# Convolutions in rounds of sixteen tiles, weights fused inside the recurrence, and TensorE's waits at the first weight load

## The reference

```python
x = x + L0(_gn(x))        # a bidirectional LSTM along one image axis, then a linear layer
x = x + L1(_gn(x))        # three convolutions joined: plain, and two with learned offsets
```

```python
out_standard = conv2d(x, conv_w, conv_b, padding=1)                     # 3x3, 32 -> 32 channels
h = relu(batchnorm(conv2d(x, dw_w, dw_b, padding=1, groups=32)))        # once for x, once for y
offset = conv2d(h, pw_w, pw_b)                                          # 32 -> 9 offsets a pixel
out_x, out_y = (einsum('bchwk,ock->bohw', bilinear_samples(x, offset), weight) for x and y)
out = relu(batchnorm(conv2d(concatenate([out_standard, out_x, out_y]), fus_w)))   # 96 -> 32, 1x1
```

## Time and profile before

| what | us |
|---|---|
| time before, median of three runs | 897.43 (894.85 to 897.92) |
| the profiled execution's own time | 896.58 |
| its span, first to last instruction | 894.1 |
| TensorE matmuls busy | 772.6 (86%) |
| VectorE busy | 615.6 (69%) |
| ScalarE busy | 478.8 (54%) |
| GpSimd busy | 249.4 (28%) |
| TensorE on the chain that ended last | 67% |

### The profile page before, as it was taken

How to read it: one execution, slowest core, us unless ns; L and a number is a source line. 1 busy time by engine, 2 the same in 40 slices (tenths; PEclk the granted TensorE clock), 3 DMA queues, 4 the chain that set the end, 5 groups by cost and what they waited for, 6 DMA issues and landing times.

```text
span 894.1 us, 61283 instructions
## 1 busy us (share of the span) xinstructions
PE 772.6 (86%) x27560; PEld 604.2 (68%) x27560; DVE 615.6 (69%) x1136; ACT 478.8 (54%) x980; POOL 249.4 (28%) x284
## 2 busy tenths in 40 slices
PE   0588888887959999959977999999999999999970
PEld 0365655554527777742257899999989999999970
DVE  4466656665461222246676898989889999999984
ACT  0344444441021111126565787878877787878754
POOL 1122222210000000000023444454445555554533
PEclk9999999997569999989999999999999999999995
DMA  8200000000000000000000000000000000000006
GB/s 222 84 3 1 0 1 0 0 1 1 1 3 4 4 4 3 4 4 1 1 4 3 0 0 0 0 0 0 0 0 0 0 0 0 0 0 0 0 1 188
DMA packets 4061, 11.96 MB, mean 13 GB/s; under 512 B 1391, under 2 KB 1787, under 8 KB 3460
## 3 DMA queue, kind: packets, MB, share of 16 engines
q1 hardware_dynamic: 1716, 4.88, 2.0%
q10 hardware_dynamic: 1522, 4.14, 1.7%
q0 software_dynamic: 768, 2.10, 0.8%
HBM read 6.92 MB, written 4.19 MB: 12 GB/s over the span
## 4 chain that ended last, share of the span: by engine, by line
PE 67%; DVE 11%; ACT 10%; issue 7%; DMA 2%; POOL 1%; ACTq 1%; DVEq 0%; POOLq 0%
PE psum L825 14%; PE psum L878 12%; PE psum L949 11%; PE psum L904 8%; ACT wide L462 6%; PE psum L763 5%; PE psum L896 5%; PE psum L848 3%; PE psum L750 3%; PE psum L805 2%; DVE offs L642 2%; DVE wide L561 2%; DVE wide L564 2%; DMA xs<-in_x_dram 2%; ACT wide L393 2%
## 5 line engine op out<-in xcount | busy, mean ns | idle before, releaser
L462 ACT ACTIVATE wide<-psum 128x512 f32<-128x512 f32 x576 | 299.5, 601 | 13.1 <-PE psum L878 6.0
L878 PE MATMUL psum<-wide,sels 125*32 125x256 bf16 x4608 | 230.2, 274 | 1.6 <-issue 1.0
L949 PE MATMUL psum<-wide 128*32 128x64 f32 x8192 | 193.3, 218 | 2.0 <-issue 2.0
L666 DVE TENSOR_SCALAR wide<-wide 128x1024 f32<-128x1024 f32 x256 | 180.1, 723 | 2.1 <-ACT wide L462 2.0
L949 PEld LDWEIGHTS psum<-wide 128*32 128x32 f32 x8192 | 168.1, 109 | 5.3 <-issue 2.6
L673 DVE COPY wide<-psum 128x1024 f32<-128x1024 f32 x128 | 155.9, 1218 | 2.0
L333 POOL COPY wide<-offs 125x256 bf16 (+1 forms) x64 | 27.1, 423 | 438.5 <-DVE offs L642 249.1
L325 POOL TENSOR_SCALAR wide<-wide 128x512 f32<-128x512 f32 x64 | 130.3, 2035 | 6.9 <-ACT wide L462 6.9
L825 PE MATMUL psum<-img,offs 32*32 32x512 f32 x3456 | 127.0, 597 | 4.4 <-DVE img L615 4.4
L763 PEld LDWEIGHTS psum<-wide 128*64 128x64 f32 x2048 | 75.6, 138 | 66.7 <-issue 65.6
L825 PEld LDWEIGHTS psum<-img,offs 32*32 32x32 f32 x3456 | 96.8, 104 | 33.7 <-issue 8.2
(11 more groups left out here) (98 smaller groups left out, 816.4 us busy)
## 6 DMA issues: line engine op xcount, KB each, us to landing
xs<-in_x_dram SPq DMA_DIRECT2D x8, 256.0 KB, 10.3
xs<-in_x_dram ACTq DMA_DIRECT2D x8, 256.0 KB, 10.9
out_dram<-wide SPq DMA_DIRECT2D x16, 128.0 KB, 3.5
out_dram<-wide POOLq DMA_DIRECT2D x16, 128.0 KB, 4.1
offs<-in_cw_dram ACTq DMA_DIRECT2D x1, 576.0 KB
sels<-in_sel_dram ACTq DMA_DIRECT2D x1, 562.5 KB
wide<-in_dsc_dram ACTq DMA_DIRECT2D x1, 288.0 KB
offs<-in_dwd_dram ACTq DMA_DIRECT2D x1, 288.0 KB
```

The source lines that it names most:

```text
L462: nc.scalar.activation(hat_tile(par, i), use_bank(par, hat_use(i)).rearrange("p (q n) -> p q n", q=2), ACT.Abs).then_inc(d_read, 1)
L666: nc.vector.tensor_scalar(v, v, 1.0, 1.0, ALU.min, ALU.subtract).then_inc(v_ready, 1)
L878: last = mm(bank[c, e * SL:(e + 1) * SL], sels[:, k, c], oc[0:NROW, par, :], start=(e == 0), stop=(e == 1))
L949: last = mm(ps[O_BANK][C * q:C * q + C, cols], w, v, start=(group == 0), stop=(group == GROUPS - 1))
```

## The change

Four things are done.

- `pe_turn` is gone, so that the wait on `h_ready[b]` stands at the first weight load of the half-step.
- ScalarE's loop over the recurrence and its loop over the convolutions are written out.
- `fuse` is called inside the last four steps of the recurrence: one tap behind each half-step but the first, seven in all, and the last two taps behind the last half-step. The results lie in banks 0 to 3. ScalarE reads them out as before, behind its own last step.
- The convolutions go in 12 rounds of four jobs. A job is a kind j and a chunk n; each round has kinds 0, 2 and 1, and a fourth job of a kind that rotates. Job i of round m uses column tiles (q + i) % 4 and bank 4 (m % 2) + i, so all sixteen tiles are used. A round waits until round m - 2 has been read out. The fourth job's result lies in other partitions than the others of its kind; for kinds 0 and 2 ScalarE reads it out in four pieces of 32 partitions, for kind 1 it stays where it is, and L848 takes it from there (`X_PLACE`). TensorE waits for both padded images before the first tap.

The diff, without its blank lines:

```diff
@@ -160,7 +160,7 @@
         h_ready = [sem(f"h_ready{b}") for b in range(2)]
         xst_ready = sem("xst_ready"); x_used = sem("x_used")
         hf_stored = sem("hf_stored"); h_stored = sem("h_stored"); h_last = sem("h_last")
-        pool_turn = sem("pool_turn"); pe_turn = sem("pe_turn")
+        pool_turn = sem("pool_turn")
         lin_ready = sem("lin_ready"); x1_ready = sem("x1_ready")
         fuse_mm = sem("fuse_mm"); zeroed = sem("zeroed"); fuse_ev = sem("fuse_ev"); pool_chain = sem("pool_chain")
         pad_zero = sem("pad_zero"); pad_ready = [sem(f"pad_ready{b}") for b in range(2)]
@@ -186,7 +186,6 @@
         UNROLL = 2 * GROUP
-        ACT_UNROLL = 2 * UNROLL
@@ -209,9 +208,25 @@
         NORM_BANK = 7
-        KINDS = 3
+        PLACES = {0: 0, 2: 1, 1: 2}
+        TURN = (0, 2, 1)
+        CONV_ROUNDS, made = [], [0, 0, 0]
+        for m in range(3 * NCH // 4):
+            kinds = (0, 2, 1, TURN[m % 3])
+            CONV_ROUNDS.append([])
+            for j in kinds:
+                CONV_ROUNDS[m].append((j, made[j]))
+                made[j] += 1
+        X_PLACE = {n: i for jobs in CONV_ROUNDS for i, (j, n) in enumerate(jobs) if j == 1}
+        def conv_bank(m, i):
+            return ps[4 * (m % 2) + i]
         ROUNDS = 4
         RC = NCH // ROUNDS
+        FUSED_AT = K * C
         block = ctx.enter_context(nc.Block())
@@ -401,32 +416,40 @@
                     gate_functions(b, j, count)
                     cell_tanh(b, count)
-            with act.Fori(0, S // ACT_UNROLL) as it:
-                for st in range(ACT_UNROLL):
-                    act_step(st % UNROLL, it * ACT_UNROLL + (st + 1))
+            for st in range(S):
+                act_step(st % UNROLL, st + 1)
             for a in range(2):
                 act.wait_ge(fuse_mm, a + 1)
                 nc.scalar.activation(wc[:, a, :], ps[a][:, 0:K * C], ACT.Copy, scale=-1.0).then_inc(fuse_ev, 1)
-            act.wait_ge(fuse_mm, 3)
             for n in range(3):
                 m = min(4, K - 4 * n) * P
-                last = nc.scalar.activation(of[:, K * P + 4 * P * n:K * P + 4 * P * n + m], ps[(2, 3, 6)[n]][:, 0:m], ACT.Copy)
-            nc.scalar.activation(cbias, ps[6][:, P:P + 1], ACT.Copy).then_inc(fuse_ev, 1)
+                at = FUSED_AT if n == 2 else 0
+                last = nc.scalar.activation(of[:, K * P + 4 * P * n:K * P + 4 * P * n + m], ps[(2, 3, 0)[n]][:, at:at + m], ACT.Copy)
+            nc.scalar.activation(cbias, ps[1][:, K * C:K * C + 1], ACT.Copy).then_inc(fuse_ev, 1)
             norm_sqrt(GN2, 2)
             act.wait_ge(norm_done, GN2 + 1)
             act.wait_ge(pad_zero, 2)
             nc.scalar.activation(pad[:, 1, 1:1 + S, 1:1 + S], xv[:, 1], ACT.Identity, bias=coef[:, GN2, 1, 1:2],
                                  scale=coef[:, GN2, 0, 1:2]).then_inc(pad_ready[1], 1)
-            with act.Fori(0, NCH // 2) as it:
-                for par in range(2):
-                    act.wait_ge(conv_mm, it * 2 + (par + 1))
-                    nc.scalar.activation(acc[:, ds(it * (2 * CH) + par * CH, CH)], ps[par][:, :], ACT.Identity,
-                                         bias=cbias[:, 0:1]).then_inc(conv_ev, 1)
-                    act.wait_ge(hy_mm, it * 2 + (par + 1))
-                    nc.scalar.activation(h_y[:, ds(it * (2 * CH) + par * CH, CH)], ps[4 + par][:, :], ACT.Identity,
-                                         bias=vecs[:, V_DWB + 1:V_DWB + 2]).then_inc(hy_ev, 1)
+            for m, jobs in enumerate(CONV_ROUNDS):
+                for i, (j, n) in enumerate(jobs):
+                    if j == 1:
+                        continue
+                    made_by, done = (conv_mm, conv_ev) if j == 0 else (hy_mm, hy_ev)
+                    to, bias = (acc, cbias) if j == 0 else (h_y, vecs[:, V_DWB + 1:V_DWB + 2])
+                    cols = slice(n * CH, (n + 1) * CH)
+                    act.wait_ge(made_by, n + 1)
+                    if i == PLACES[j]:
+                        last = nc.scalar.activation(to[:, cols], conv_bank(m, i)[:, :], ACT.Identity, bias=bias[:, 0:1])
+                    else:
+                        for q in range(Q):
+                            at, own = C * ((q + i) % Q), C * ((q + PLACES[j]) % Q)
+                            last = nc.scalar.activation(to[own:own + C, cols], conv_bank(m, i)[at:at + C, :], ACT.Identity,
+                                                        bias=bias[at:at + C, 0:1])
+                    last.then_inc(done, 1)
             norm_sqrt(BN, 2)
             def relu_image(b):
@@ -615,14 +638,21 @@
             nc.vector.tensor_scalar(pad[:, 0, 1:1 + S, 1:1 + S], xv[:, 0], coef[:, GN2, 0, 0:1],
                                     coef[:, GN2, 1, 0:1], ALU.mult, ALU.add).then_inc(pad_ready[0], 1)
-            for n in range(NCH):
-                v = h_x[:, n * CH:(n + 1) * CH]
-                dve.wait_ge(hx_mm, n + 1)
-                nc.vector.tensor_scalar(v, ps[2 + n % 2][:, :], vecs[:, V_DWB:V_DWB + 1], None, ALU.add).then_inc(hx_ev, 1)
-                dve.wait_ge(hy_ev, n + 1)
-                nc.vector.bn_stats(stats_hy[:, n, :], h_y[:, n * CH:(n + 1) * CH])
-                dve.wait_ge(hx_ev, n + 1)
-                last = nc.vector.bn_stats(stats[:, n, :], v)
+            for m, jobs in enumerate(CONV_ROUNDS):
+                for i, (j, n) in enumerate(jobs):
+                    if j == 1:
+                        v = h_x[:, n * CH:(n + 1) * CH]
+                        dve.wait_ge(hx_mm, n + 1)
+                        nc.vector.tensor_scalar(v, conv_bank(m, i)[:, :], vecs[:, V_DWB:V_DWB + 1], None, ALU.add
+                                                ).then_inc(hx_ev, 1)
+                for j, n in jobs:
+                    if j == 2:
+                        dve.wait_ge(hy_ev, n + 1)
+                        last = nc.vector.bn_stats(stats_hy[:, n, :], h_y[:, n * CH:(n + 1) * CH])
+                for j, n in jobs:
+                    if j == 1:
+                        dve.wait_ge(hx_ev, n + 1)
+                        last = nc.vector.bn_stats(stats[:, n, :], h_x[:, n * CH:(n + 1) * CH])
             step(last)
             nc.vector.bn_aggr(mv[:, 0, :], stats[:, :, :])
             step(nc.vector.bn_aggr(mv[:, 1, :], stats_hy))
@@ -755,7 +785,6 @@
             def gates_h(b, j, count):
                 pe.wait_ge(h_ready[b], count)
-                pe.sem_inc(pe_turn, 1)
                 gates = stream_gates(b, j)
                 for g in range(4):
                     for d in range(2):
@@ -785,44 +814,58 @@
             with pe.Fori(1, NG // 2 - 1) as it:
                 for st in range(UNROLL):
                     pe_step(st, it * UNROLL + (st + 1), it * 2 + (st // GROUP + 2))
-            for st in range(UNROLL):
-                pe_step(st, S - UNROLL + st + 1, NG if st < GROUP else None)
+            FUSED = (2, 3, 0)
             def fuse(t):
+                at = FUSED_AT if t == K - 1 else (t % 4) * P
+                mm(ps[FUSED[t // 4]][:, at:at + P], cw_s[:, t, :], fus_s, start=(t % 4 == 0 and t < K - 1), stop=(t % 4 == 3))
+                if t == K - 1:
+                    mm(ps[1][:, K * C:K * C + 1], fus_s, vecs[:, V_CONVB:V_CONVB + 1], start=False, stop=False)
                 for a in range(2):
                     last = mm(ps[a][:, t * C:(t + 1) * C], dsc_s[:, a, t, :], f23_s[:, a, :], start=(t == 0), stop=(t == K - 1))
                     if t == K - 1:
                         last.then_inc(fuse_mm, 1)
-                mm(ps[(2, 3, 6)[t // 4]][:, (t % 4) * P:(t % 4 + 1) * P], cw_s[:, t, :], fus_s, start=(t % 4 == 0),
-                   stop=(t % 4 == 3))
+            for st in range(GROUP):
+                pe_step(st, S - UNROLL + st + 1, NG)
             pe.wait_ge(conv_in, 16 * 7)
+            taps = 0
+            for st in range(GROUP, UNROLL):
+                for b in range(2):
+                    gates_h(b, st, S - UNROLL + st + 1)
+                    if (st, b) != (GROUP, 0):
+                        fuse(taps)
+                        taps += 1
+            while taps < K:
+                fuse(taps)
+                taps += 1
             pe.wait_ge(h_stored, 2 + NG - 1)
             pe.wait_ge(h_last, 1)
             for n in range(NCH):
                 pe.wait_ge(x1_ready, 2 * n + 2)
                 mm(ps[4 + n % 2], wlin_s, seq[:, n * 4 * SEQ:(n + 1) * 4 * SEQ], start=True, stop=True).then_inc(lin_ready, 1)
-                if 1 <= n <= K:
-                    fuse(n - 1)
-            mm(ps[6][:, P:P + 1], fus_s, vecs[:, V_CONVB:V_CONVB + 1], start=False, stop=True).then_inc(fuse_mm, 1)
             norm_mm(GN2, 2)
             pe.wait_ge(fuse_ev, 3)
-            for n in range(NCH):
-                b, r0 = n // (NCH // 2), n % (NCH // 2) * ROWS
-                if r0 == 0:
-                    pe.wait_ge(pad_ready[b], 1)
-                if n >= 2:
-                    pe.wait_ge(conv_ev, n - 1)
-                    pe.wait_ge(hx_ev, n - 1)
```

(20 more changed lines are left out.)

## The result

Four runs of the kernel before took 896.8 us (median; 894.85 to 897.92), four of the changed one 857.14 (856.93 to 857.33): a ratio of 0.956, 95% interval 0.9542 to 0.9578. The forecast was 856.0. The profiled execution took 857.32 us with a span of 855.5, at a mean granted clock of 0.969.

The account below looks back on a forecast made before the run. Recurrence bound by latency, linear stage by TensorE at half clock, convolutions by TensorE alone. Terms -3.6 - 4.2 + 2.7 - 20.5 + 1.4 - 17.1 + 0.8 = -40.5 took 896.58 to 856.1, predicted 856; range 850 to 861.

Parts of the forecast that it names:

- Part 1: Recurrence: no increment behind the hidden state's wait, 0.06 us for 60 steps, -3.6 us; bounds 0 and -6.
- the floor I had read: Recurrence: ScalarE alone was said to set a floor of 2.32 us for a step of both streams.
- Part 2: Recurrence: ScalarE's loop written out saves three activation table loads, -4.2 us; bounds -3.1 to -6.5.
- Part 3: Last four recurrence steps: fusing taps lengthen half-steps from 1.19 to 1.55 us, +2.7 us; bounds +1 to +5.
- Part 4: Linear stage without fusing: full clock at entry, VectorE as bound, 24.1 us for 44.6, -20.5 us.
- Part 5: Before the first convolution tap: waiting for both padded images, ScalarE's taking 3.82 us against VectorE's 2.42, +1.4 us.
- Part 6: Convolutions on sixteen tiles: 108 taps for 144, 0.99 us a tap at full clock, 109.5 us, -17.1 us.
- the hold: Convolutions: a weight load of pass k waits until matmul k - 33 has ended, a 64-instruction queue emptied in order.
- Full concurrency: Rival, convolutions: the hold on loads is slack somewhere; conv 95.6 us, in all 842; chance 0.27.
- No gain from the fourth tile: Rival, convolutions: a shared limit, such as reads or weight loads, 1.15 us a tap; conv 126, in all 872; chance 0.10.
- A low clock all through the linear stage: Rival, linear stage: half clock stays, +5.3 us, about 861; chance 0.10, shared with dear fusing in the recurrence.
- The slower case: Rival, convolutions: fourth stream in a row group waits for three others, 1.72 us a tap, in all 932; chance 0.03.

Follow-up runs that it names:

- fuse_linear: Changed kernel with the nine taps of the weights' fusing moved back between the linear matmuls, none in the recurrence: 874.94 us.
- fuse_linear_busy: Changed kernel with the nine fusing taps back between the linear matmuls, and three unread matmuls filling TensorE's gap ahead of the linear stage: 862.18 us.
- late_wait: Changed kernel with the wait for the second padded image moved to the first round that reads it: median 857.35 us, ratio 0.9571.
- late_warm4: Changed kernel with the second image's wait at its first reading round, and unread matmuls around the norm's two, four in front: median 852.45 us, ratio 0.9528.
- twelve: Changed kernel with sixteen convolution rounds of three jobs on twelve tiles, instead of twelve rounds of four: 869.87 us.
- after_again: The changed kernel itself, unedited, run once more beside later runs: median 857.24 us, ratio 0.9569.

## Why the prediction was right, and where its sizes were off

All signs held, and the stages from the recurrence to the offsets' first matmul give -38.5 in sum, where it forecast -40.5; start-up gave 2.0 and the start of the sampling took 1.9, which cancel by chance. That the whole came out within 1.2 us of 856 is in part luck too: the convolutions gave 2.7 less than forecast, and the fall of the clock in the recurrence of the kernel before, which is no part of the change, made up 1.2 of it.

- **Part 1, increment.** Forecast -3.6, and 4.2 when put back alone. The floor is not ScalarE alone but its loop with VectorE, 2.30 us in the steps that it sets, 0.02 below the floor I had read.
- **Part 2, table loads.** Forecast -4.2; put back alone, 2.8 us. The step that failed is the price of 2.2 for the second load, from a stretch with a second cause in it. The two together were to give -7.8; put back one by one they are worth 7.0.
- **Part 3, half-steps.** 1.59 us against 1.55 + 0.1 forecast. The forecast's sum is 2.16 + 0.6 = 2.8, where I wrote 2.7. From the ninth-last start of ScalarE's gate function to the first linear matmul it took 212.38 - 199.60 = 12.78 us before and 204.35 - 189.43 = 14.92 after, both at full clock but for the end of before's gap: 2.1 more, with nine half-steps' share of part 1 in it, so that the fusing alone costs 2.1 to 2.6 (6 x (1.59 - 1.15) = 2.6), near the forecast. The row of the recurrence agrees: -4.2 - 2.8 - 1.2 for the clock + 2.2 = -6.0. `fuse_linear`'s recurrence, 165.48, is only 1.6 shorter than after's because its last steps ran at half clock.
- **Part 4, linear stage.** 24.01 against 24.1, at full clock, with VectorE as the bound. `fuse_linear` and `fuse_linear_busy` separate its two causes.
- **Part 5, both images.** +1.4 forecast, +1.35 in the trace. `late_wait` took 1.47 back.
- **Part 6, sixteen tiles.** -17.1 forecast, -14.4 measured. The mechanism held: the single load of the next tap in the trace after, and the reversed orders. The mis-sized term is the tap: 1.013 us against 0.99. Over the 101 taps from the seventh start to the last that is 2.3 us; the first six taps took 8.60 us against 5.4 + 3 x 0.99 = 8.37, another 0.2; the last tap lasts 1.69 from its start to the end of its last matmul, where I had counted a tap and 0.15, another 0.55. Together 3.1, which is 112.58 - 109.5. The stage's half clock lasts as long as chance has it: with the same tap the six other executions took 111.19 to 112.39, 1.7 to 2.9 over 109.5. My half-clock tap of 1.83 was too long (1.68 to 1.71): the hold is not there from the start, since at full clock too the first two taps take 0.86 and 0.89 and only the third 1.04 (`late_warm4`). Three taps and most of a fourth, 1.38, went at the lower clock.
- **The rivals.** Full concurrency (842) falls by 1.013 against 0.858; so does the reading of the Trainium skill (TensorE: Matmul & The Clock Gate, Part 3, Measured speedup vs the span model) that one pack of sixteen costs a matmul and 4 ns a tile, once packs follow each other; Part 1 there, the queue of 64 with weight loads pulled ahead, agrees with the 32 loads and the one. No gain from the fourth tile (872) falls by `twelve` at 869.87. A low clock all through the linear stage (+5.3) came in no execution with the taps moved out; the 3.4 us of it in `after_again` cost 1.3. The slower case asked for 1.38 a tap.

A tap costs 0.858 / 12 = 0.0715 us for each tile at twelve tiles and 1.013 / 16 = 0.0633 at sixteen: 11% less, where full concurrency had promised 25%. By the stepped rule, an estimate, 14 tiles would take 0.878 a tap and 15 tiles 0.94, both 0.0627 a tile, where it has 0.997 / 16 = 0.0623 for sixteen: no gain in sight, and not tried.

## What to carry to other kernels

When independent tiles are issued round-robin on an in-order queue, count how many instructions lie between a tile's two uses, and compare that with the queue: here 24 passes were free, 32 cost 18% a tap, and only the order of issue made 12 tiles lose what 16 did. Before a stage with a throttled clock, look at what TensorE does in the last microseconds ahead of it and fill an idle gap there with work that has to be done anyway, since the clock that a stage enters with can stay for all of it: this was worth 16 of 40 us. Where a whole time scatters by 1.5 us, read an edit of 1 us in its own stage of the trace, look at the granted clock of both sides of the comparison before a difference is put down to the edit, and do not add up what cancels.

## What the runs showed of the hardware

- **The queue.** Weight loads run ahead of matmuls only as far as the queue is emptied, and it is emptied in program order: 32 loads, then 1, then 31, of which the second came 0.03 us after matmul 2 had ended. Same matmuls in another order: 0.858 to 1.017 us a tap on 12 tiles, 1.013 to 1.085 on 16.
- **The clock keeps its level.** 30 us of TensorE 100% busy with alternating matmuls of 512 columns and the small ones of a tap stayed at 0.51 (`fuse_linear`), and the same at 1.00 (`fuse_linear_busy`). Which one depended on whether TensorE idled for 2.62 us ahead or worked through matmuls of 512 columns; in both the clock had been at half before that, from 195.1 us on.
- **The clock also falls with no cause that the code shows**, TensorE being busy all the while that it is down: at the linear stage's start from 204.8 to 208.2 us in one execution of the changed kernel and not in another, and from 129.8 to 133.2 us in the recurrence of the kernel before alone.
- **A table reload in a loop** occupies ScalarE for 1.28 us and costs 0.93 on the path, for a set that does not change.
- **Scatter without a cause in the code:** start-up 36.9 to 39.2 us, the first six half-chunks of the sampling 45.2 to 49.8.
